# Moving the quad's projections, the weighing and the splits within the slots of a four-transformer chain

## The reference

```python
def _attn(q, k, v, mask):                 # block L0: self attention (mask), then cross attention (mask)
    s = jnp.einsum('bqhd,bkhd->bhqk', q, k) * scale
    s = jnp.where(mask, s, jnp.finfo(s.dtype).min)
    a = jax.nn.softmax(s, axis=-1)
    return jnp.einsum('bhqk,bkhd->bqhd', a, v)
...
# block L2: cross attention, queries from x, keys and values from the context, both after ada_ln
scores = jnp.einsum('bqhd,bkhd->bhqk', q, k) / jnp.sqrt(jnp.float32(dh))
attn = jax.nn.softmax(scores, axis=-1)
...
# block L3: self attention, cross attention, feed-forward
x = x + mha(xn, xn, xn, ...)
x = x + mha(x, u, u, ...)
```

## Time and profile before

| | |
|---|---|
| median of 3 runs | 1069.88 us (1067.48 to 4715.3) |
| the profiled execution | 1063.98 us, its span 1061.8 us |
| PE busy | 971.6 us, 91% |
| DVE, ACT, POOL busy | 749.7, 623.6, 616.5 us |
| mean granted clock of TensorE | 0.952 |
| chain that ended last, by engine | PE 68%, DVE 14%, issue 8%, POOL 7% |

### The profile page before, as it was taken

How to read it: one execution, slowest core, us unless ns; L and a number is a source line. 1 busy time by engine, 2 the same in 40 slices (tenths; PEclk the granted TensorE clock), 3 DMA queues, 4 the chain that set the end, 5 groups by cost and what they waited for, 6 DMA issues and landing times.

```text
span 1061.8 us, 32084 instructions
## 1 busy us (share of the span) xinstructions
PE 971.6 (91%) x13009; PEld 670.9 (63%) x13009; DVE 749.7 (71%) x1852; ACT 623.6 (59%) x938; POOL 616.5 (58%) x739
## 2 busy tenths in 40 slices
PE   7898898998889999999999988888999998888998
PEld 5455565666566776676776655655666666566676
DVE  7767888777875444677787768877898766776421
ACT  2144455577767555545554567775677677775752
POOL 6657888576874332111113779776778655685520
PEclk9569999999997999999999989998999999997999
DMA  6613333434332102000000133333334333333011
GB/s 215 219 65 112 120 108 107 133 107 134 125 120 74 41 30 98 9 10 7 7 7 19 59 116 107 123 107 103 131 112 145 116 125 119 110 98 121 7 40 40
DMA packets 101459, 96.89 MB, mean 91 GB/s; under 512 B 11632, under 2 KB 93808, under 8 KB 100928
## 3 DMA queue, kind: packets, MB, share of 16 engines
q1 hardware_dynamic: 101312, 94.84, 26.9%
HBM read 18.77 MB, written 2.15 MB: 20 GB/s over the span
## 4 chain that ended last, share of the span: by engine, by line
PE 68%; DVE 14%; issue 8%; POOL 7%; ACT 1%; SPq 1%; DMA 0%; POOLq 0%; DVEq 0%; ACTq 0%
PE weighed L725 13%; DVE negmax L1242 8%; PE row_scores L658 8%; PE scores L921 6%; PE weighed L748 5%; PE scores L613 4%; PE row_scores L921 3%; PE quads L620 3%; POOL kblk_r L1952 3%; PE quads L594 2%; PE row_scores L738 2%; PE scores L738 2%; PE quads L605 2%; PE row_scores L634 2%; PE weighed L938 2%
## 5 line engine op out<-in xcount | busy, mean ns | idle before, releaser
L1242 DVE TENSOR_REDUCE negmax<-row_scores 128x8 f32<-128x616 f32 (+1 forms) x312 | 298.5, 957 | 101.4 <-PE row_scores L658 74.4
L1758 ACT ACTIVATE p<-scores 128x1024 f32<-128x1024 f32 (+1 forms) x253 | 253.1, 1019 | 123.4 <-PE scores L710 87.7
L1952 POOL TENSOR_TENSOR kblk_r<-work,pack_const 128x308 fp32r<-128x308 f32 (+1 forms) x160 | 133.6, 836 | 113.0 <-PE row_scores L658 92.1
L658 PE MATMUL row_scores<-kblk_r,qr 32*128 32x308 f32 (+1 forms) x624 | 145.5, 457 | 52.4 <-DVE negmax L1242 42.4
L725 PE MATMUL weighed<-p,v 77*32 77x128 f32 (+1 forms) x5120 | 184.4, 288 | 1.8 <-DVE nat L1258 1.3
L725 PEld LDWEIGHTS weighed<-p,v 77*32 77x32 f32 (+1 forms) x5120 | 137.9, 114 | 36.1 <-issue 27.2
L658 PEld LDWEIGHTS row_scores<-kblk_r,qr 32*128 32x128 f32 x624 | 63.9, 191 | 130.2 <-issue 84.6
L695 PE MATMUL scores<-q_ring,k_ring 32*77 32x128 f32 (+1 forms) x2512 | 123.0, 256 | 4.4 <-ACT shared L1695 1.7
L695 PEld LDWEIGHTS scores<-q_ring,k_ring 32*77 32x77 f32 (+1 forms) x2512 | 100.0, 167 | 7.9 <-ACT shared L1695 1.9
L1258 DVE STREAM_TRANSPOSE nat<-weighed 128x256 f32<-128x256 f32 x160 | 70.9, 443 | 41.8 <-PE weighed L725 37.1
L710 PE MATMUL scores<-nblk,select 32*77 32x512 bf16 (+1 forms) x628 | 93.1, 396 | 0.0
(11 more groups left out here) (334 smaller groups left out, 1958.1 us busy)
## 6 DMA issues: line engine op xcount, KB each, us to landing
q_ring<-work SPq DMA_DIRECT2D x160, 128.0 KB, 2.1
q_ring<-qr SPq DMA_DIRECT2D x160, 128.0 KB, 2.1
k_ring<-k_high SPq DMA_DIRECT2D x64, 128.0 KB, 2.1
k_ring<-work SPq DMA_DIRECT2D x64, 128.0 KB, 2.1
k_ring<-k_high SPq DMA_DIRECT2D x96, 77.0 KB, 2.0
k_ring<-work SPq DMA_DIRECT2D x96, 77.0 KB, 2.0
shared<-gates_hbm SPq DMA_DIRECT2D x24, 256.0 KB, 3.1
shared<-in_ctx_tok SPq DMA_DIRECT2D x15, 154.0 KB
```

The source lines that it names most:

```text
L658: mm = e.matmul(row_banks(n, h)[:, i, 0:cols], qr[q % 3][at, s * S:(s + 1) * S], kblk_r[n % 2][at, 0:cols], start=layer.mask is None or ma ...
L1242: e.tensor_reduce(negmax[q % 2][:, 2 * h:2 * h + 2, s * NJ:(s + 1) * NJ], row_banks(n, h)[:, :, 0:NJ * nk].rearrange("p g (j k) -> p g j k ...
L1758: e.activation(p[n % 2][0:nk, 8 * h:8 * h + 8, :], score_banks(n, h)[0:nk].rearrange("p g (j q) -> p (g j) q", j=NJ), ACT.Exp, bias=hide, ...
L1952: e.tensor_tensor(kblk_r[n % 2][:, 0:NJ * nk].rearrange("p (j k) -> p j k", j=NJ), k_of[q % 2][:, s * nk:(s + 1) * nk].unsqueeze(1).to_bro ...
```

## The change

PE, wide slots: all of `quad_work` but `project_v` stands between the subtractions and the row scores of t+6; `project_v` (cl 2) and `weigh` follow the row scores. In masked slots the second half of the score mask (`mask_scores(t, 1)`) comes right after the subtractions, no longer beside the row mask. PE, narrow slots: `weigh` of job t-1 stands between the subtractions and the row scores of t+6, and `quad_work` stays behind them. POOL: `split_q` and `split_k` of quad qi+2 move from cl 3 to cl 0 of the next quad, except for the first quad of a phase.

```diff
                 def quad_work(t, qi, cl):
                     early = max(min(2 * t + 1, 8 * hi), 8 * lo)
-                    if cl == 2 and qi + 1 in quads:
+                    if cl == 2 and qi + 1 in quads and not (t in jobs and layer_of(qi).nk == S):
                         w.wait_ge(exp_done, early)
                         project_v(qi + 1)
...
-                    rest = slice(2 if is_wide(t) else 0, QUAD)
                     if cl == 0 and qi + 2 in quads and t != -2 * QUAD:
-                        project_k(qi + 2, rest)
+                        project_k(qi + 2)
...
-                    if cl == 2 and qi - 2 in quads and not is_wide(t):
+                    if cl == 2 and qi - 2 in quads:
...
-                    if cl == 3 and qi + 3 in quads and not (is_wide(t) and layer_of(qi).rope):
-                        project_q(qi + 3, rest)
+                    if cl == 3 and qi + 3 in quads:
+                        project_q(qi + 3)
...
                         exact(t)
                         shift(t, 0)
                         shift(t, 1)
-                    if is_wide(t):
-                        quad_ahead(qi, cl)
-                    if phase == 1 and t in (4 * lo - 2, 4 * lo - 1):
-                        keep_busy(4, av_bank[:, 0:128])
-                    if t + 6 in jobs:
-                        rows(t + 6, 0)
                     if masked:
-                        mask_rows(t + 6, 0, False)
                         mask_scores(t, 1)
                         if cl == 3 and qi + 1 in quads:
                             w.wait_ge(nblk_done, qi + 2)
-                    if masked or is_wide(t) and cl == 2:
+                    if phase == 1 and t in (4 * lo - 2, 4 * lo - 1):
+                        keep_busy(4, av_bank[:, 0:128])
+                    if t == 4 * hi:
+                        first_layer(phase, 0, hi, range(2))
+                    wide = t in jobs and layer_of(qi).nk == S
+                    if wide:
                         quad_work(t, qi, cl)
-                        if t - 1 in jobs:
-                            weigh(t - 1)
-                    else:
-                        if t == 4 * hi:
-                            first_layer(phase, 0, hi, range(2))
-                        if t - 1 in jobs:
-                            weigh(t - 1)
-                        if t + 6 in jobs:
-                            mask_rows(t + 6, 0, False)
-                        if t in (-6, -4, -3):
-                            keep_busy(3, scores[:, 0, 0:128])
-                        if cl == 3 and qi + 1 in quads:
-                            turn_max(qi + 1)
+                    elif t - 1 in jobs:
+                        weigh(t - 1)
+                    if t + 6 in jobs:
+                        rows(t + 6, 0)
+                        mask_rows(t + 6, 0, False)
+                    if wide and cl == 2 and qi + 1 in quads:
+                        w.wait_ge(exp_done, max(min(2 * t + 1, 8 * hi), 8 * lo))
+                        project_v(qi + 1)
+                    if wide and t - 1 in jobs:
+                        weigh(t - 1)
+                    if t in (-6, -4, -3):
+                        keep_busy(3, scores[:, 0, 0:128])
+                    if not masked and cl == 3 and qi + 1 in quads:
+                        turn_max(qi + 1)
+                    if not wide:
                         quad_work(t, qi, cl)
...
                     if t - 2 in jobs:
                         normalise(t - 2)
-                    if cl == 3 and qi + 2 in quads:
-                        split_q(qi + 2)
-                        split_k(qi + 2)
+                    if t == 4 * lo - 5:
+                        split_q(lo)
+                        split_k(lo)
+                    if cl == 0 and qi + 1 in quads and qi + 1 != lo:
+                        split_q(qi + 1)
+                        split_k(qi + 1)
```

11 lines of the change are left out of this document (removed).

## The result

| | before | after |
|---|---|---|
| median | 1069.38 us | 1202.55 us (1194.32 to 1209.47) |
| ratio, 95% interval | 1 | 1.125 (1.115 to 1.135) |
| span of the profiled execution | 1061.8 us | 1207.3 us |
| mean granted clock | 0.952 | 0.846 |
| PE, DVE, ACT, POOL busy | 971.6, 749.7, 623.6, 616.5 us | 1089.6, 745.4, 618.5, 618.2 us |

The account below looks back on a forecast made before the run. PE is near the bound, with two cycles setting it: the single row-score buffer and the rings' lap. 1064 + 21 (l0) + 14 (narrow lap) + 12.5 (l3s) = 1111, plus 19 for the clock: 1130 us, range 1098 to 1162.

Parts of the forecast that it names:

- The transposes of xh in l0: In l0, splits directly ahead of xh make PE wait about 2.9 us; cost 2.75 us a quad, 21 with the mask overall.
- The lap in narrow quads: In narrow quads, later splits delay the transfers: two quads take 32.3 us, 16.15 each; loss 0.7 a quad, 14 us overall.
- Projections ahead in wide slots at 0.3 us for the mask and nothing else: Wide slots: projections ahead of row scores cost nothing in l3s; in l0 the second score mask costs 0.3 us alone.
- weighing ahead at no loss: Narrow slots: weighing fills a 0.51 us wait per slot, freeing 1.2 us a quad, which turns into PE's wait for exact scores.
- the term of 12.5 us: In l3s, the same lap takes 36.4 us for two quads, 18.2 each against 16.6: 8 x 1.6 = 12.5 us.
- The clock: Waits of 1.7 to 3 us in every quad invite falls to 1.2 GHz, each costing PE 1.5 to 2.75 us; 19 us taken.
- Rival B: The clock stays low: once at half clock PE may not win it back for long; 1164 to 1190 us, chance 0.14.

Follow-up runs that it names:

- e8: Changed kernel plus idle matmuls: 8 ahead of cl 0's exact scores in narrow quads, 10 ahead of l0's xh transposes, none in l3s; 1147.91 us, ratio 1.073.
- e7: Changed kernel issuing only 8 of a quad's 16 transfers from the fourth pair of jobs on; 1128.11 us, ratio 1.058.
- e6: Kernel before with only PE's new order in wide slots, narrow slots and splits as before; 1087.42 us, ratio 1.019.
- e5: Kernel before with only the weighing moved ahead of the row scores in narrow slots; 1084.99 us, ratio 1.017.
- e9: Kernel before with weighing ahead in narrow slots, plus 5 idle matmuls ahead of cl 0's exact scores in narrow quads; 1068.66 us, ratio 1.002.
- e13: As e8, with l3s filled too: 10 idle matmuls ahead of the xh transposes, 8 ahead of cl 0's exact scores; 1137.32 us, ratio 1.067.
- e14: Kernel before with one added PE wait per quad of l3s, at cl 1, for the next quad's first pair of transfers; 1096.01 us, ratio 1.029.
- e4: Changed kernel plus 20 idle matmuls ahead of xh transposes in wide slots, 16 ahead of cl 0's exact scores from quad 8; 1204.54 us, ratio 1.125.

## Why the prediction was right and wrong

**The transposes of xh in l0: right.** Wait 2.9 forecast, 3.14 measured; a quad at full clock 23.8 forecast, 23.57 in e8. That e8's l0 is 20.7 us above before, against 21, is partly luck: it spent 14 us at half clock there, the kernel before 27.

**The lap in narrow quads: right.** First issue 3.26 us behind the first exponential (3.2 to 3.4), quads at full clock 16.0 to 16.6 (16.15), the rounding's wait at 47.6 us (40 or more), and e7 removed it. With the clock held (e8) the wait comes in every quad, as forecast. In the changed kernel it comes 17 times in all and in l3c in every second quad, because the quads between are at half clock; that shape is the clock's, not the lap's.

**Projections ahead in wide slots at 0.3 us for the mask and nothing else, weighing ahead at no loss: too small.** e6 loses 1.9% and e5 1.7%. e5's full-clock quads, at 14.4 to 14.7 us, show that the weighing fills its wait; what was left out is that PE's idle time, collected ahead of the exact scores, is met by the clock. e5's quad 10 and e9 show it; the long stretch at the start of phase 1 stays unexplained, and so does e6's loss beyond l0.

**l3s: the term of 12.5 us was too small.** With the clock at 1.00, e13's l3s takes 156.0 us, 24.6 above before, fill included. Quads 24 to 28 wait for an `xh` behind the splits, the same queue of POOL as in l0, and I applied that step to l0 alone. It is 11.4 us of waits in e7, and 11.4 in the changed kernel too (five of 2.3); the prediction has no term for it. The lap's own term was not far off: quads 29 to 31, without such a wait, take 1.9 us more than before on average, against 1.6.

**The clock: the failed step.** "A fall to 1.2 GHz so costs 1.5 to 2.75 us of PE" was read from windows one slot long, and most falls last longer than a slot. (Of the 2.75, 2.26 is PE's busy time; the rest is a wait.) In the changed kernel's attention 24 falls begin, against 7 before, and 15 of them last 10 us or more, up to 20; a further stretch of 44 us runs into l2 from just before it, where it was 10. In e14 a fall added 1.6 us to PE's busy time when it lasted 3.4 us and 4.6 to 5.5 when it lasted 10 to 14, somewhat under half its length. The number of falls was not the error: 19 us stood for two thirds of 33 quads paying once, 22 falls, and 17 more than before came. Instead 349 us passed at 1.2 GHz, PE was busy 120 us longer, some 7 us for each new fall (an estimate, 120 by 17), and e13 puts at least 61 us of the time on the clock. Rival B, at 0.14, named this mechanism ("may not win it back for long") and was itself too low with 1164 to 1190. The argument against it, that the falls of the earlier trace rows were over within a slot or two, rested on the two windows chosen. The same trace has longer ones; three of its seven falls in the attention look like this:

```profile
315.90:329.60 13.70, 13.51 (x180) 10.34 (x180) 6.57 (x20) 6.80 (x10) 5.08 (x8) 0.50 0.39 125
616.30:626.40 10.10, 10.03 (x122) 7.25 (x122) 6.60 (x24) 5.28 (x9) 6.29 (x9) 0.50 0.47 152
971.20:984.90 13.70, 13.44 (x178) 10.44 (x178) 6.67 (x20) 6.25 (x10) 6.82 (x9) 0.50 0.39 124
```

So the right price could have been read before the change.

Of the 67 us by which the loss was underestimated (133 against 66), about 42 are the clock's (61 against 19) and about 25 the waits' (72 against 47.5), by e13, whose fill shifts some of the first to the second. The order of the two shares is not in doubt; their sizes are a lower value for the clock's and an upper one for the waits'. One slip besides, without weight: the lowest run of the kernel before is 3.5 us above the profiled execution, not 3.6.

## What to carry over

Where an engine's idle time is cheap because it lies in many short pieces, a reordering that gathers it into one piece can cost more than it frees. Price a wait of TensorE by the whole stretch at the lower clock behind it, taken from a timeline until the durations are back, and not by the slot in which it starts; and look through all such stretches of the trace before taking one as the price. When work is moved behind other work on a helper engine, list every reader of that engine's queue in every layer, not only in the layer where the move was seen first.

## What was not expected of the hardware

A wait of PE of the same 2.5 us, eight times in the same code, was followed by half clock four times, and the price was then 1.6 us once and 4.6 to 5.5 three times (e14). Adding matmuls that compute nothing ahead of a wait made a kernel faster, from a ratio of 1.125 to one of 1.073 (e8), and by too many of them nothing was gained (e4). The Trainium skill ("TensorE: Matmul & The Clock Gate", What's actually happening) puts the ramp, in which the first matmuls run at the low clock, under 1% of a typical kernel's span. Here the clock fell again and again behind waits, and this cost more: the stretches at 1.2 GHz in the five layers were 29% of the span (349 of 1207 us) and cost at least 5% of the time (61 us, e13).
